# Two LoRA layers on 2048 rows: adapter numbers spread by TensorE, x1, x2 and layer 1's rows loaded ahead of A, three places for transposed x, row ends stored first with a gather of their own

## The chip, the cores and the metric

One core of a Trainium2 chip. The time is what the device takes for one execution, in microseconds; before the change it is 98.39 us, the median of 3 runs (98.32 to 98.45).

## The reference

```python
# x: (64, 32, 512) f32; itok_B_6_15: (64,), adapters 6 to 15 of 32; itok_B_3_7: (64,), adapters 3 to 7 of 8; rank 16
# layer 0
result = einsum('bsd,od->bso', x, base_weight) + base_bias
h = einsum('bsd,brd->bsr', x, lora_A_w[itok_B_6_15])
x = x + result + einsum('bsr,bor->bso', h, lora_B_w[itok_B_6_15])
# layer 1
Bx = einsum('bni,bri->bnr', x, B[itok_B_3_7])
x = x + einsum('bnr,bor->bno', Bx, A[itok_B_3_7])     # SCALING is 1
```

Each of the 64 batches has 32 rows of 512 numbers and one adapter for each layer.

## The kernel before

The 2048 rows are 16 blocks of 128 rows, that is of 4 batches. Both layers are folded into one product: with W+ = weight + identity, the result of a block is x W+^T, plus for every row a rank part of 32 columns for its batch (16 of layer 0 and 16 of layer 1). For layer 1 the factor B1 has to be applied to x W+^T; that product (`c1`) is made once at the start, and so is the product of B1 with lora_B (`g`), which carries layer 0's rank part into layer 1's.

Every fp32 value is held as a high and a low fp32r part, and each product is three matmuls (high by high, high by low, low by high). ACT writes high parts (`copy`, its line is L558), DVE low parts (`low`, L640).

For a block k TensorE does:
- `base(k)` (L394): the transposed x (`xt`, two places in turn) against W+ in two halves of 256 columns; one of the halves has 128 more columns, the block's chosen adapter rows (`select` on ACT, layers L0 and L1), so 384 columns.
- `add_gh(k)` (L432): `u_own` (on DVE, from the 128 columns, turned and masked) against `g_sel(k)`, which GpSimd selects from the gathered rows (`g_select`, L332).
- `up(k)` (L440): 6 matmuls of the rank part (`u_sel`) against `up_rows`, whose high part is `up_high` on ACT and low part `up_low` on GpSimd (L339).
Then DVE adds the bias (`finish`, L679) and SyncE (SP) stores the block.

The order of each engine is written out by hand. In the steady loop TensorE does add_gh(k-1) behind the first quarter of base(k), and up(k-1) behind base(k). add_gh(2) stands in base(3), behind up(1).

The gathered rows come from a table in DRAM, `by_rank`, of 640 rows (40 adapters by 16 ranks) of 644 numbers: 512 of lora_B or of layer 1's A (by rank), then the row's end: 128 of `g` (or of the identity, for layer 1), and one of bias times B1. `by_rank` is stored at the start by SP: four stores of lora_B (`bw_by_rank`), four of A1 (`a1_by_rank`), and one of all row ends (`row_ends`, L223), which waits for `g` and its copy on ACT. All nine count on one semaphore. GpSimd waits for all of it and issues one indirect DMA for each block (`gather`, L322), 128 rows of 2,576 bytes, 330 KB; four places (GATHERS). gather(0), (1), (2) go ahead of the loop, in which come g_select(k), up_low(k) and gather(k+3). The numbers of the rows to gather are computed on GpSimd (L291 to L314) from `ids_all`, which two DMAs spread over 128 partitions.

At the start TensorE runs 6 `keep_warm` matmuls on zeros (L362), b1's transposes, the four `w_fill` (transposes of W+, L370) with `c1_part` between them (L378), `x_fill(0)` (transposes of x, L414), lora_B's transposes (L466), x_fill(1), base(0)'s first half, the 16 matmuls of `g` (L480), the transposes of A (L487), base(1)'s second half, x_fill(2), base(0)'s second half, and so on. An fp32 matmul is counted as two by the profile, a transpose as one. base(0)'s second half is begun without the chosen columns, and `down` (L405) adds them for the first two chunks once ACT has selected them. Blocks from 3 on are transposed by DVE (`x_turn`, L647).

SP issues its DMAs in one queue, in the order written: b1, w (4), x0, lora_B, lora_A, x1, A1, x2, ids (2), bias, the nine stores, x3, then the rest of x between the stores of the output.

## Time and profile before

| | |
|---|---|
| median of the runs | 98.39 us (98.32 to 98.45) |
| the profiled execution's own time | 97.92 us |
| its span | 95.8 us |
| busy: TensorE, its weight loads | 91.5 us, 90.0 us |
| busy: DVE, ACT, GpSimd (POOL) | 64.8 us, 58.7 us, 58.0 us |
| share of TensorE in the chain that ended last | 90% |
| moved by DMA | 19.45 MB, mean 203 GB/s |

The span runs from the first instruction to the last, and the time has some 2 us more around it. The chain is followed back from the last instruction, at each step to what released it or to the instruction ahead of it on its engine.

### The profile page before, as it was taken

What the parts mean: (1) busy time and instruction counts of PE and PEld (TensorE: products, weight loads), DVE (VectorE), ACT (ScalarE), POOL (GpSimd) and SP (SyncE); (2) the same over time, 40 slices, a digit from 0 to 9 for tenths busy, and PEclk for the clock granted to TensorE, in tenths of its full rate; (3) what the DMA queues carried; (4) which work ended last, traced back from release to release, by engine and by line L of the source; (5) the groups of instructions that cost most, each with busy time, mean ns of one, the idle gap of its engine ahead of it and who ended that gap; (6) DMA issues with size and microseconds to landing.
All of it is one profiled execution on the core that took longest, in us unless ns stands there. A gap on an engine that the chain in (4) does not pass through costs nothing.

```text
span 95.8 us, 2305 instructions
## 1 busy us (share of the span) xinstructions
PE 91.5 (96%) x662; PEld 90.0 (94%) x662; DVE 64.8 (68%) x120; ACT 58.7 (61%) x189; POOL 58.0 (61%) x126
## 2 busy tenths in 40 slices
PE   5999999999999999999999999999999999999980
PEld 5899999999899998999999999999999999999970
DVE  4499799227076468959587877768595868786460
ACT  0074598874588796748494948567584949480210
POOL 6504008850568999999576584959585766808500
PEclk9999999999999999999999999999999999999998
DMA  2999998968896289989996499992836354520205
GB/s 40 312 347 387 374 403 262 281 156 214 215 224 223 53 250 238 310 249 235 203 290 218 70 319 209 238 269 91 228 44 229 34 213 54 200 110 0 110 0 219
DMA packets 16335, 19.45 MB, mean 203 GB/s; under 512 B 1444, under 2 KB 11556, under 8 KB 16164
## 3 DMA queue, kind: packets, MB, share of 16 engines
q1 hardware_dynamic: 15040, 14.04, 50.1%
q0 software_dynamic: 1280, 5.28, 22.1%
q8 instruction: 5, 0.08, 0.4%
q14 instruction: 6, 0.05, 0.3%
q10 hardware_dynamic: 4, 0.00, 0.0%
HBM read 13.47 MB, written 5.84 MB: 202 GB/s over the span
## 4 chain that ended last, share of the span: by engine, by line
PE 90%; DVE 4%; ACT 2%; issue 1%; DVEq 0%; ACTq 0%
PE psum L394 55%; PE psum L440 11%; PE psum L432 4%; PE psum L362 4%; PE psum L480 4%; PE psum L378 4%; PE psum L370 3%; DVE table_rounded L640 3%; PE psum L466 2%; PE psum L414 1%; PE psum L405 1%; PE psum L448 1%; DVE y L679 1%; ACT row_ends L558 1%; ACT table_rounded L558 1%
## 5 line engine op out<-in xcount | busy, mean ns | idle before, releaser
L394 PE MATMUL psum<-wd,xt 128*128 128x256 f32 (+1 forms) x384 | 62.3, 310 | 0.0
L394 PEld LDWEIGHTS psum<-wd,xt 128*128 128x128 f32 x384 | 56.1, 188 | 0.0
L558 ACT ACTIVATE wd<-table_rounded 128x128 fp32r x128 | 27.7, 297 | 14.7 <-PE psum L394 12.5
L339 POOL TENSOR_TENSOR up_rows<-gathered_rows,up_rows 128x512 fp32r<-128x512 f32 x16 | 20.6, 1289 | 14.0 <-ACT up_rows L558 14.0
L322 POOL DMA_INDIRECT gathered_rows<-by_rank,rows x16 | 15.9, 996 | 6.3 <-DMA by_rank<-row_ends 3.8
L640 DVE TENSOR_TENSOR xt<-psum,xt 128x512 fp32r<-128x512 f32 x16 | 11.1, 691 | 6.6 <-ACT xt L558 5.9
L647 DVE STREAM_TRANSPOSE psum<-x_squares 128x512 f32<-128x512 f32 x13 | 14.4, 1110 | 0.0
L440 PE MATMUL psum<-up_rows,u_sel 128*128 128x256 f32 x96 | 14.2, 284 | 0.0
L440 PEld LDWEIGHTS psum<-up_rows,u_sel 128*128 128x128 f32 x96 | 12.8, 190 | 0.2
L659 DVE STREAM_TRANSPOSE psum<-psum 128x128 f32<-128x128 f32 x16 | 5.3, 330 | 11.2 <-PE psum L394 7.8
L332 POOL TENSOR_TENSOR g_sel<-gathered_rows,batch_mask 128x16 f32<-128x16 f32 x64 | 12.1, 227 | 0.9 <-DMA gathered_rows<-by_rank,rows 0.7
L558 ACT ACTIVATE xt<-psum 128x512 fp32r<-128x512 f32 x16 | 9.6, 597 | 4.4 <-DVE psum L647 1.8
L679 DVE TENSOR_TENSOR y<-psum,bias_all 128x512 f32<-128x512 f32 x15 | 10.4, 692 | 1.1 <-PE psum L440 0.5
L558 ACT ACTIVATE up_rows<-gathered_rows 128x512 fp32r<-128x512 f32 x16 | 10.0, 623 | 0.0
L558 ACT ACTIVATE u_sel<-psum 128x128 fp32r<-128x128 f32 x16 | 4.2, 262 | 5.8 <-PE psum L432 5.8
L432 PE MATMUL psum<-u_own,g_sel 128*128 128x128 f32 x32 | 6.3, 279 | 0.1
L640 DVE TENSOR_TENSOR u_sel<-psum,u_sel 128x128 fp32r<-128x128 f32 x16 | 4.6, 288 | 2.3 <-ACT u_sel L558 2.3
L666 DVE SCALAR_TENSOR_TENSOR u_own<-psum,gathered_rows,batch_mask 128x128 f32<-128x128 f32 x16 | 5.6, 348 | 0.5
L432 PEld LDWEIGHTS psum<-u_own,g_sel 128*128 128x128 f32 x32 | 5.3, 188 | 0.5 <-issue 0.5
L281 POOL COPY a_by_rank<-a_rows 128x1024 f32<-128x1024 f32 x1 | 2.0, 2010 | 5.3 <-DMA a_rows<-in_L_cond_A 5.3
L362 PE MATMUL psum<-warm 128*128 128x128 f32 x16 | 3.9, 425 | 1.1 <-DVE warm L683 1.1
L362 PEld LDWEIGHTS psum<-warm 128*128 128x128 f32 x16 | 3.6, 330 | 1.1 <-DVE warm L683 1.1
(60 smaller groups left out, 72.1 us busy)
## 6 DMA issues: line engine op xcount, KB each, us to landing
out<-y SPq DMA_DIRECT2D x15, 256.0 KB
x_squares<-in_x SPq DMA_DIRECT2D x8, 256.0 KB
w_rows<-in_L_cond_base_weight SPq DMA_DIRECT2D x4, 256.0 KB, 4.0
bw_rows<-in_L_cond_lora_B_w SPq DMA_DIRECT2D x1, 1024.0 KB, 7.0
a_rows<-in_L_cond_lora_A_w SPq DMA_DIRECT2D x1, 1024.0 KB, 9.2
by_rank<-bw_by_rank SPq DMA_DIRECT2D x4, 256.0 KB
x_squares<-in_x SPq DMA_DIRECT2D x8, 128.0 KB
x_rows<-in_x SPq DMA_DIRECT2D x3, 256.0 KB, 9.3
```

What stands on the lines that cost most here:

```text
L322: nc.gpsimd.indirect_dma_start(out=gathered_rows[:, k % GATHERS, :], out_offset=None, in_=by_rank_dram[:, :], in_offset=bass.IndirectOffse ...
L332: last = nc.gpsimd.tensor_tensor(out=g_sel[:, k % 2, b, L1, :], in0=gathered_rows[:, k % GATHERS, bass.ds(n1[b] * R + G_COL, R)], in1=batc ...
L339: nc.gpsimd.tensor_tensor(out=up_rows[:, k % 2, LO, :], in0=gathered_rows[:, k % GATHERS, 0:D], in1=up_rows[:, k % 2, HI, :], op=ALU.subtr ...
L362: nc.tensor.matmul(XT[:, 0:P], warm[:, :], warm[:, :], start=True, stop=True)
L394: last = nc.tensor.matmul(bank_of(k, half)[:, start:end], xt[:, k % 2, c, x_part, :], wd[:, w_part, c, col:col + end - start], start=(c == ...
L432: nc.tensor.matmul(u_now, g_sel[:, k % 2, :, :, :], u_own[:, :], start=True, stop=True).then_inc(gh_filled, 1)
L440: last = nc.tensor.matmul(products(k)[:, half, :], u_sel[:, k % 2, u_part, :], up_rows[:, k % 2, r_part, half * HALF:(half + 1) * HALF], s ...
L558: return nc.scalar.activation(dst, src, ACT.Copy)
L640: return nc.vector.tensor_tensor(out=dst, in0=whole, in1=high, op=ALU.subtract)
L647: nc.vector.transpose(out=XT.rearrange("p (c b s) -> p b c s", c=C, b=NB), in_=x_squares[:, k * NB:(k + 1) * NB, :].rearrange("p b (i c) - ...
L666: nc.vector.scalar_tensor_tensor(out=u_own[:, :], in0=u_blocks, scalar=gathered_rows[:, k % GATHERS, BB_COL:BB_COL + 1], in1=batch_mask[:, ...
L679: nc.vector.tensor_tensor(out=y[:, k % SLOTS, :].rearrange("p (h n) -> p h n", h=2), in0=products(k), in1=bias_all[:, :].rearrange("p (h n ...
```

## The change

- The adapter numbers of both layers are scaled on one partition by DVE (`ids_scaled`) and spread over 128 partitions by one matmul with ones; the two DMAs of `ids_all` go. DVE copies the result out of PSUM, and GpSimd computes the row numbers ahead of w_chunks(3), no longer behind the bias terms.
- 5 warm-up matmuls instead of 6, the 2 fillers go. b1's copy goes from DVE to ACT, and a small ACT operation (`table_call`) stands ahead of it.
- SP loads x1 and x2 ahead of A1, and bias and A (`lora_A`) behind them.
- `xt` has three places. x_fill(2) stands ahead of the matmuls of `g`, base(2)'s first half ahead of base(0)'s second, which is now one piece of 12 matmuls of 384 columns; `down` goes.
- A row of `by_rank` is now its end first (132 numbers, 16 unused), then the 512: 660 numbers, five units of 132. `row_ends` is stored ahead of the four stores of A1, on a semaphore of its own, and block 0's ends are gathered by themselves (`first_ends`, 528 bytes a row) as soon as it has landed. gather(0) waits for the rest of the table; then g_select(0), then gather(1), (2), (3).
- up_low(0) goes from GpSimd to DVE; ACT does u_high(0) ahead of up_high(0).
- x's fifth group of blocks (4 and 5) is cut in two.

SP's queue from the bias load to x's later groups. Before:

```order
L212 DMA bias_all<-in_L0_cond_base_bias 128x512
L182 DMA by_rank<-bw_by_rank 512x1x128 [waits bw_by_rank_ready]
L182 DMA by_rank<-bw_by_rank 512x1x128 x3
L182 DMA by_rank<-a1_by_rank 128x1x128 [waits a1_by_rank_ready]
L182 DMA by_rank<-a1_by_rank 128x1x128 x3
L223 DMA by_rank<-row_ends 128x5x132 [waits act_drained,bias_b1_ready,zeros_ready]
L194 DMA x_squares<-in_x 32x4x128 x4
L194 DMA x_squares<-in_x 32x8x128 x4
```

The same place after the change:

```order
L239 DMA bias_all<-in_L0_cond_base_bias 128x512
L240 DMA a_rows<-in_L0_cond_lora_A_w 128x4x512
L213 DMA by_rank<-bw_by_rank 512x1x128 [waits bw_by_rank_ready]
L213 DMA by_rank<-bw_by_rank 512x1x128 x3
L250 DMA by_rank<-row_ends 128x5x148 [waits act_drained,bias_b1_ready,zeros_ready]
L213 DMA by_rank<-a1_by_rank 128x1x128 [waits a1_by_rank_ready]
L213 DMA by_rank<-a1_by_rank 128x1x128 x3
L225 DMA x_squares<-in_x 32x4x128 x8
```

The row ends' store has passed the four of A1, and lora_A stands behind the bias.

GpSimd at its first gathers, before (ISA rows set a register for the one behind them):

```order
L322 DMA gathered_rows<-by_rank,rows 128x644 [waits masks_ready,table_stored,ids_in,rows_ready]
L322 DMA gathered_rows<-by_rank,rows 128x644 x2
L241 TENSOR_LOAD ids
L332 ISA [waits gathered_0]
L332 TENSOR_TENSOR g_sel<-gathered_rows,batch_mask 128x16
```

and after:

```order
L379 DMA first_ends<-by_rank,first_units 128x132 [waits masks_ready,ends_stored,ids_in,rows_ready]
L355 DMA gathered_rows<-by_rank,rows 128x660 [waits table_stored]
L272 TENSOR_LOAD ids
L365 ISA [waits first_ends_gathered]
L365 TENSOR_TENSOR g_sel<-first_ends,batch_mask 128x16
L365 ISA
L365 TENSOR_TENSOR g_sel<-first_ends,batch_mask 128x16
L365 ISA
L365 TENSOR_TENSOR g_sel<-first_ends,batch_mask 128x16
L365 ISA
L365 TENSOR_TENSOR g_sel<-first_ends,batch_mask 128x16
L355 DMA gathered_rows<-by_rank,rows 128x660 x3
```

A gather has come ahead of the others, and g_select(0) stands between gather(0) and gather(1).

TensorE from base(1)'s second half to add_gh(0), before:

```order
L394 MATMUL psum<-wd,xt 128x256 x11
L414 MATMUL psum<-ident,x_rows 128x128 [waits x_loaded_2,xt_lo_ready]
L414 MATMUL psum<-ident,x_rows 128x128 x3
L394 MATMUL psum<-wd,xt 128x256 [waits dve_drained,act_drained]
L394 MATMUL psum<-wd,xt 128x256 x5
L405 MATMUL psum<-wd,xt 128x128 [waits sel1_ready,sel0_ready]
L405 MATMUL psum<-wd,xt 128x128 x5
L394 MATMUL psum<-wd,xt 128x384 x6
L394 MATMUL psum<-wd,xt 128x384 [waits sel0_ready,sel1_ready,dve_drained,act_drained]
L394 MATMUL psum<-wd,xt 128x384 x11
L394 MATMUL psum<-wd,xt 128x256 [waits xt_lo_ready,xt_hi_ready]
L394 MATMUL psum<-wd,xt 128x256 x11
```

and after:

```order
L433 MATMUL psum<-wd,xt 128x256 [waits act_drained,xt_lo_ready,xt_hi_ready]
L433 MATMUL psum<-wd,xt 128x256 x11
L433 MATMUL psum<-wd,xt 128x256 [waits act_drained,dve_drained,xt_lo_ready,xt_hi_ready]
L433 MATMUL psum<-wd,xt 128x256 x11
L433 MATMUL psum<-wd,xt 128x384 [waits sel0_ready,sel1_ready,dve_drained,act_drained]
L433 MATMUL psum<-wd,xt 128x384 x11
L433 MATMUL psum<-wd,xt 128x384 [waits sel0_ready,sel1_ready,dve_drained,act_drained]
L433 MATMUL psum<-wd,xt 128x384 x11
L462 MATMUL psum<-u_own,g_sel 128x128
```

The transposes and the six matmuls of 128 columns are gone from here, and block 2's first half stands ahead of block 0's second. The core of the diff:

```diff
-WARM_UPS = 6
-FILLERS = 2
+X_SLOTS = 3
+WARM_UPS = 5
-G_COL, BB_COL = D, D + P
-ROW = BB_COL + 4
+G_COL, BB_COL = 0, P
+ENDS = P + 4
+UNITS = 5
+ROW = UNITS * ENDS
+UP_AT = ROW - D
...
-            sp.dma_start(a_rows[:, :, :], lora_a.rearrange("(g n) r d -> (n r) g d", g=C)).then_inc(a_in, 16)
             load_x(1)
+            load_x(2)
...
-            load_x(2)
-            for layer, ids_of in ((L0, ids0), (L1, ids1)):
-                sp.dma_start(ids_all[:, layer, :, :].rearrange("p k b -> p (k b)"),
-                             ids_of.rearrange("(a k) -> a k", a=1).to_broadcast([P, B])).then_inc(ids_all_in, 16)
             sp.dma_start(bias_all[:, :], bias.rearrange("(a n) -> a n", a=1).to_broadcast([P, D])).then_inc(bias_in, 16)
+            sp.dma_start(a_rows[:, :, :], lora_a.rearrange("(g n) r d -> (n r) g d", g=C)).then_inc(a_in, 16)
...
+            sp.dma_start(by_rank_dram.rearrange("(g p) c -> p g c", p=P)[:, :, 0:UP_AT], row_ends[:, :, :]).then_inc(ends_stored, 16)
             sp.wait_ge(a1_by_rank_ready, 2)
             for c in range(C):
                 store_by_rank(sp, a1_by_rank, N1, N0 * R, c)
-            sp.dma_start(by_rank_dram.rearrange("(g p) c -> p g c", p=P)[:, :, D:ROW], row_ends[:, :, :]).then_inc(table_stored, 16)
...
+            nc.gpsimd.tensor_scalar(out=first_units[:, :], in0=row_sums[:, 0:1], scalar1=float(UNITS), scalar2=None,
+                                    op0=ALU.mult).then_inc(rows_ready, 1)
...
-            pool.wait_ge(table_stored, (2 * C + 1) * 16)
+            pool.wait_ge(ends_stored, 16)
+            nc.gpsimd.indirect_dma_start(out=first_ends[:, :], out_offset=None,
+                                         in_=by_rank_dram.rearrange("n (u c) -> (n u) c", c=ENDS),
+                                         in_offset=bass.IndirectOffsetOnAxis(ap=first_units[:, 0:1], axis=0),
+                                         ).then_inc(first_ends_gathered, 16)
+            pool.wait_ge(table_stored, 2 * C * 16)
             gather(0)
+            g_select(0)
             gather(1)
             gather(2)
-            for k in range(NBLK):
+            gather(3)
+            for k in range(1, NBLK):
...
+            pe.wait_ge(ones_ready, 1)
+            pe.wait_ge(ids_scaled_ready, 1)
+            nc.tensor.matmul(fill_of("ids")[:, 0:2 * B], ones[:, :], ids_scaled[:, :],
+                             start=True, stop=True).then_inc(filled, 1)
             w_fill(0)
-            keep_warm(FILLERS)
...
             base(0, range(C), halves=[0])
+            x_fill(2)
...
             base(1, range(C), halves=[1])
-            x_fill(2)
+            wait_x(2)
+            wait_drained(pe, "a0")
+            base(2, range(C), halves=[0])
             wait_drained(pe, "c1")
-            base(0, [0, 1], halves=[1], with_d=False, group_check=False)
             wait_d(0)
-            down(0, [0, 1])
-            base(0, [2, 3], halves=[1], group_check=False)
+            base(0, range(C), halves=[1])
...
-            wait_x(2)
-            base(2, range(C), halves=[0])
             add_gh(0)
             wait_d(2)
-            base(2, [0, 1], halves=[1])
+            base(2, range(0, C - 1), halves=[1])
             up(0)
-            base(2, [2, 3], halves=[1])
+            base(2, [C - 1], halves=[1])
...
             select(1, L0, first[1, L0])
-            xt_high(2)
             select(2, L0)
             select(2, L1)
-            up_high(0)
             xt_high(3)
             u_high(0)
+            up_high(0)
             select(3, L0)
             up_high(1)
             select(3, L1)
...
             turn_u(0)
-            xt_low(2)
+            own_u(0)
             x_turn(3)
-            own_u(0)
             xt_low(3)
             u_low(0)
             turn_u(1)
+            dve.wait_ge(up_hi_ready, 1)
+            low(up_rows[:, 0, LO, :], gathered_rows[:, 0, UP_AT:ROW], up_rows[:, 0, HI, :]).then_inc(first_up_ready, 1)
             own_u(1)
```

## Rows read from the trace of the kernel before

**Rows 1.** The page's busy time (us), share of the span, instructions.

```profile
PE 91.5 (96%) x662; PEld 90.0 (94%) x662; DVE 64.8 (68%) x120; ACT 58.7 (61%) x189; POOL 58.0 (61%) x126
```

**Rows 2.** Windows: stretch, length, busy time (instructions) by engine, PEclk, DMA share, GB/s.

```profile
36.20:92.00 55.80, 55.80 (x405) 55.80 (x406) 40.55 (x77) 35.39 (x127) 38.46 (x77) 1.00 0.69 177
```

**Rows 3.** The chain that ended last: start us, us, what.

```profile
1.12 2.93 PE psum L362 x12
...
6.73 0.89 PE psum L378 x8
...
10.85 0.48 PE psum L414 x4
...
14.06 0.72 PE psum L414 x4
14.77 1.43 PE psum L394 x12
16.20 3.58 PE psum L480 x32
...
24.21 0.30 ACT wd L558
...
25.44 4.65 PE psum L394 x30
30.09 0.24 PE psum L432 x2
...
36.19 0.46 PE psum L432 x2
```

**Rows 4.** Timeline of POOL: start us, us, line, operation [idle before it <- what ended it].

```profile
18.15 0.19 POOL L291 CAST row_of_rank_f<-row_of_rank 128x8 f32<-128x8 int32 x1
...
20.66 0.20 POOL L314 CAST rows<-row_sums 128x16 uint32<-128x16 f32 x1
24.63 1.16 POOL L322 DMA_INDIRECT gathered_rows<-by_rank,rows  x1 [3.77 <-DMA by_rank<-row_ends]
26.10 0.95 POOL L322 DMA_INDIRECT gathered_rows<-by_rank,rows  x1 [0.30 <-issue]
...
28.96 0.77 POOL L332 TENSOR_TENSOR g_sel<-gathered_rows,batch_mask 128x16 f32<-128x16 f32 x4 [0.66 <-DMA gathered_rows<-by_rank,rows]
...
31.13 0.99 POOL L322 DMA_INDIRECT gathered_rows<-by_rank,rows  x1
32.13 0.76 POOL L332 TENSOR_TENSOR g_sel<-gathered_rows,batch_mask 128x16 f32<-128x16 f32 x4
32.84 1.28 POOL L339 TENSOR_TENSOR up_rows<-gathered_rows,up_rows 128x512 fp32r<-128x512 f32 x1
34.28 0.99 POOL L322 DMA_INDIRECT gathered_rows<-by_rank,rows  x1 [0.16 <-POOL up_rows L339]
35.28 0.76 POOL L332 TENSOR_TENSOR g_sel<-gathered_rows,batch_mask 128x16 f32<-128x16 f32 x4
```

**Rows 5.** DMA issues: number, KB of one, median us from issue to landing.

```profile
b_rows<-in_L_cond_B SPq DMA_DIRECT2D x1, 256.0 KB, 2.7
```

**Rows 6.** Timeline of ACT.

```profile
19.81 0.60 ACT L558 ACTIVATE row_ends<-psum 128x512 f32<-128x512 f32 x1 [0.90 <-PE psum L480]
...
31.61 0.61 ACT L558 ACTIVATE up_rows<-gathered_rows 128x512 fp32r<-128x512 f32 x1
32.13 0.90 ACT L558 ACTIVATE wd<-table_rounded 128x128 fp32r x4
```

**Rows 7.** Timeline of TensorE: base(1)'s second half, behind A's transposes.

```profile
21.46 1.68 PE L394 MATMUL psum<-wd,xt 128*128 128x256 f32 x12
```

**Rows 8.** Timeline of SP, its DMA issues.

```profile
17.34 2.56 SPq L182 DMA_DIRECT2D by_rank<-a_by_rank  x4
20.51 0.38 SPq L223 DMA_DIRECT2D by_rank<-row_ends  x1
20.94 4.02 SPq L194 DMA_DIRECT2D x_squares<-in_x  x8
```

More of the change, by code:

```diff
@@ L171, in wait_drained, with ends, wait_ends, wait_up_rows @@
                 engine.wait_ge(dve_drained, DVE_DRAINS.index(name) + 1)
+        def ends(k, col, width):
+            if k == 0:
+                return first_ends[:, bass.ds(col, width)]
+            return gathered_rows[:, k % GATHERS, bass.ds(col, width)]
+        def wait_ends(engine, k):
+            if k == 0:
+                engine.wait_ge(first_ends_gathered, 16)
+            else:
+                engine.wait_ge(gathered[k % GATHERS], 16 * (k // GATHERS) + 16)
+        def wait_up_rows(engine, k):
+            if k == 0:
+                engine.wait_ge(first_up_ready, 1)
+            else:
+                engine.wait_ge(up_ready, k)
         def chunk(rows_of, c):
@@ L457, in _ @@
             c1_part(1)
+            wait_drained(pe, "ids")
             w_fill(3)
@@ L717, in _, with lay_bw @@
             xt_low(0)
-            for q in range(4):
+            def lay_bw(q):
                 wait_filled(dve, f"bw{q}")
```

147 lines of the change are left out of this document (79 added, 68 removed).

## The prediction

> **What bounds the kernel now.** I read first the page's busy shares: TensorE is busy for 96% of the span [rows 1]. Then its share after the start: from 36.2 us to 92.0 it is busy for all of 55.80 us [rows 2], so no other engine and no transfer costs anything there, and that stretch keeps its order. What the change can move is the time at which it begins, that is the third add_gh, at 36.19 us in the chain that ended last [rows 3]. So the question is one number: where does that matmul land afterwards?
>
> The same chain tells what comes before it [rows 3]. TensorE runs nearly without a hole, but slowly at first: 12 warm-up passes take 2.93 us (0.24 each), while 8 passes from 6.73 us on take 0.89 (0.111 each). x_fill(1) takes 0.72 where another x_fill takes 0.48, so it waits 0.24 for x1 at 14.06; and the chain leaves TensorE at 19.79 for ACT and DVE, to come back from the adapter selection at 24.51.
>
> Last, GpSimd's timeline from 24.63 to 36.04 us, which the chain doesn't show [rows 4]. GpSimd waits for the store of row_ends, then works almost solidly: three gathers, a wait of 0.66 for the first to land, and then g_select, up_low and gather in turn. g_select(2) ends at 35.28 + 0.76 = 36.04, and add_gh(2), which reads it, begins at 36.19. So TensorE fully loaded and GpSimd fully loaded arrive at that point together: an earlier TensorE alone buys nothing there.
>
> **The change part by part.** The sum is made against the profiled execution (97.92 us, of which 95.8 are the span). The median of the runs is 98.39, 0.47 above it; I add each difference to the median.
>
> Start of TensorE. One warm-up (2 passes) and two fillers (4) go, one matmul for the ids (2) comes: 4 passes fewer. They should leave no hole: b1 lands 2.7 us after its issue [rows 5], and 10 slow passes from 1.12 last until 3.6. They come out of the end of the slow part, so I price them at the fast 0.111: -0.44 (at the slow 0.24 it would be -0.98, and nothing if TensorE's faster passes began later by as much). x1 now goes ahead of the 1 MB of A, so its 0.24 goes. x_fill(2) comes ahead of the row-end matmuls: +0.48; what hides its wait is that xt_low(1) is put ahead of the last bw copy on DVE. The row ends' copy on ACT, at 19.81 for 0.60 [rows 6], moves by -0.44 - 0.24 + 0.48 = -0.20.
>
> Selection and the merged block. From 21.46 us [rows 7] TensorE now has 24 matmuls of 256 columns (0.119 each, 12 in 1.43) and 24 of 384 (18 of them in 4.65 - 1.43, so 0.179 each): 2.86 + 4.30 = 7.16 us instead of 30.09 - 21.46 = 8.63 [rows 3, 7]. base(2)'s first half fills what was a wait for select(0, L0): that ends at 24.51 - 0.20 = 24.31, TensorE gets there at 21.26 + 2.86 = 24.12, so 0.2 of waiting stays. add_gh(0) could start at 28.6 instead of 30.09: 1.5 us earlier. The third place for transposed x and the ids by TensorE cost nothing else: the small GpSimd operations on the row numbers (18.15 to 20.86 us, 2.7 in all [rows 4]) move ahead of w_chunks(3); begun at about 5.7, behind the ids' copy on DVE, they end at 8.6 with the one that is new, and leave 2.7 us for one copy before TensorE has done x_fill(0) at 10.85 + 0.48 [rows 3].
>
> The gathers. This is where it is given back. The store of row_ends is issued at 20.51 and GpSimd's first gather starts at 24.63 [rows 4, 8], 4.12 later. With the copy 0.20 earlier the same store frees GpSimd at 24.43. What stood before this store, the stores of a1, now stands behind it, with x3 and x4 (8 issues took 4.02 us [rows 8]) after them; the a1 stores take 2.56 us to issue [rows 8] and still land before GpSimd is through with the ends gather. That gather comes first: it starts at 24.43, and its landing is e later. The full gather(0) goes out behind it, at no cost, under the wait. But g_select(0) now stands ahead of gather(1), where before gather(1) followed gather(0) by 1.47 us [rows 4]. So gather(1) starts at 24.43 + e + 0.76 (g_select) + 0.15 (the gap of gathers behind GpSimd's work) and lands g later, and g_select(1) waits for it, which it did not before: it ran at 32.13, at once behind gather(3).
>
> Neither e nor g stands in the trace by itself. For g the nearest row is the first gather of the same 330 KB: start 24.63, g_select at 28.96 after its wait, 4.33. Below it is bounded by the 256 KB load of b1, 2.7 from issue to landing; above I allow 4.7. I take 4.33. For e, 66 KB instead of 330, the bounds are 2.7 and the 4.33 of the full one; I take 2.8, near the small one, because four fifths of the bytes are gone. Then gather(1) lands at 24.43 + 2.8 + 0.91 + 4.33 = 32.47.
>
> From its landing there are two ways to add_gh(2). By GpSimd: from g_select(1)'s start to g_select(2)'s end is 36.04 - 32.13 = 3.91, with 0.15 to TensorE [rows 4]: 36.6 with the wait's release. By ACT, which also stood free of gather(1) before: up_high(1) 0.61 and select(3, L1) 0.90 [rows 6] plus 0.1, then base(3) chunk 0 (0.90), up(1) (6 x 0.119 = 0.72) and chunk 1 (0.90) on TensorE: 32.47 + 4.13 = 36.6 as well. So add_gh(2) comes at 36.6 instead of 36.19: +0.4 us. The 1.5 us that TensorE gained turn into waits at up(0), add_gh(1), base(3) and add_gh(2), about 1.9 in all. up_low(0), moved to DVE, takes 1.28 off GpSimd, but the time is spent waiting for the landing of gather(1).
>
> What the Trainium skill makes of e: its page "DMA: Bandwidth & Descriptors", section "Anatomy of one DMA — SWDGE (gpsimd) path", gives a DMA a fixed cost of about 2.0 us whatever its size, plus the bytes at 436 GB/s. So a gather of a fifth of the rows is hardly shorter. As an estimate by that page, with the generation times of the rows (1.16 and 0.95) ahead, e is 1.16 + 2.0 + 0.15 = 3.3 and g 0.95 + 2.0 + 0.78 = 3.7; the sum e + g is 7.0 against my 7.13, and the result +0.3. For the first gather that page gives 3.9 where the row has 4.33.
>
> **The rivals.** All are one formula: add_gh(2) = 24.43 + e + g + 5.04; it is level with before at e + g = 6.7.
> Faster, 97.9: the gathers land sooner. Below e + g = 6.5 the kernel is faster, and what then holds it is GpSimd's own order: ends gather 1.46 with its gap, gather(0) 0.95, g_select 0.76, three gathers 3 x 1.25, so g_select(1) at 31.5 at the earliest, 0.6 ahead of 32.13, and 97.8. For it: after the changed start fewer x loads run beside gather(1), while the 4.33 was measured among them. Against it: the single measured landing.
> Level, 98.4: e + g between 6.5 and 6.9, or the start gains 0.3 to 0.4 more than I give it because the slow passes are the ones saved.
> The whole of TensorE's gain stays, 96.9: the row_ends store would have to free GpSimd 1.9 us sooner than I say. Nothing in the rows shows its 4.12 us held up by what was ahead of it, so I give it little.
> Much slower, 99.6 and over: e near the 4.33 of a full gather, which is 1.5 us more: 100.3.
>
> **How the numbers follow.** Slower as forecast, 98.8: 0.50 (0.06 of it over 99.5). Level: 0.24. Faster by gathers that land early: 0.22; the whole gain: 0.04. This kernel's runs can tell about 0.2% (0.2 us) from no change, so faster 0.26, same 0.24, slower 0.50. The forecast is 98.39 + 0.41 = 98.8. Its own range is 98.6 to 99.5; with the other cases up to the limit of GpSimd's order, 97.8 to 99.5.
>
> **What would show it.** TensorE ready for add_gh(0) at about 28.6; row_ends' copy at about 19.6 and GpSimd's ends gather at about 24.4; g_select(0) at 27.2 and gather(1) at 28.1; g_select(1) not behind gather(3) without a gap, but after a wait for gathered_rows, at about 32.5; up_high(1) on ACT at the same time; add_gh(2) at 36.6, and after it no idle TensorE and the same 55.8 us. I am wrong if g_select(1) follows gather(3) with no wait, if the ends gather starts well before 24.4, or if TensorE still has new holes after add_gh(2).

## The result, and the profile after

| | before | changed |
|---|---|---|
| median of the runs, same chip | 98.42 us (98.32 to 98.57, 4 runs) | 99.95 us (99.25 to 101.38, 4 runs) |
| ratio to before | | 1.0137 [1.0090, 1.0183] |
| the profiled execution's own time, its span | 97.92, 95.8 us | 99.41, 97.6 us |
| start of add_gh(2) | 36.19 us | 37.31 us |
| from there to add_gh(15), the last | 54.63 us | 55.23 us |

Slower, as forecast, but by 1.5 us instead of 0.4, and outside the range. In the profiles two things make up the difference: add_gh(2) came 0.7 us later than forecast, and the loop after it takes 0.6 us more (forecast: the same). A third, which neither of these two profiles shows, lifts many executions of the changed kernel by up to 2 us more. Against the three stands 0.25 us that the changed kernel takes less outside the span (1.86 on the mean against 2.11), which the forecast did not have.

The medians are over all executions, while the ratios leave out those more than 1.5% above the same kernel's fastest, which takes away most of the upper cluster where the times of a kernel fall into two, so each range is given beside its ratio.

The page's busy times of the changed kernel, as [rows 1]:

```profile
PE 92.0 (94%) x652; PEld 89.3 (92%) x652; DVE 65.3 (67%) x122; ACT 60.9 (62%) x191; POOL 58.7 (60%) x127
```

Windows, as [rows 2], but with TensorE's columns alone: stretch, length, busy time (instructions), PEclk, DMA share, GB/s. 1.39 us of holes before the loop, none in it.

```profile
24.60:38.20 13.60, 12.21 (x74) 1.00 0.72 199
38.20:94.00 55.80, 55.80 (x404) 1.00 0.72 180
```

The chain that ended last, as [rows 3]:

```profile
1.70 4.42 DMA w_rows<-in_L_cond_base_weight
6.47 0.69 DVE w_chunks L746
7.52 0.75 PE psum L410 x4
...
15.62 0.73 PE psum L444 x4
16.35 3.76 PE psum L516 x32
20.14 0.61 ACT row_ends L594
20.84 2.93 DMA by_rank<-row_ends
23.84 0.81 issue
24.66 3.38 DMA first_ends<-by_rank,first_units
29.22 3.63 DMA gathered_rows<-by_rank,rows
34.61 1.06 PE psum L433 x6
...
45.80 2.64 PE psum L433 x18
```

Where before TensorE alone led to add_gh(2), now the store of the row ends and the two gathers do. The loop's pieces come behind them.

POOL's timeline, as [rows 4]:

```profile
24.66 1.19 POOL L379 DMA_INDIRECT first_ends<-by_rank,first_units  x1 [8.42 <-DMA by_rank<-row_ends]
26.15 0.95 POOL L355 DMA_INDIRECT gathered_rows<-by_rank,rows  x1 [0.30 <-issue]
28.23 0.75 POOL L365 TENSOR_TENSOR g_sel<-first_ends,batch_mask 128x16 f32<-128x16 f32 x4 [1.13 <-DMA first_ends<-by_rank,first_units]
29.22 0.99 POOL L355 DMA_INDIRECT gathered_rows<-by_rank,rows  x1 [0.24 <-issue]
...
33.04 0.58 POOL L365 TENSOR_TENSOR g_sel<-gathered_rows,batch_mask 128x16 f32<-128x16 f32 x3 [0.33 <-DMA gathered_rows<-by_rank,rows]
33.79 0.22 POOL L365 TENSOR_TENSOR g_sel<-gathered_rows,batch_mask 128x16 f32<-128x16 f32 x1 [0.16 <-issue]
```

The order of the forecast: g_select(0) waits for the small gather, gather(1) goes out only behind it, and g_select(1) waits for gather(1).

ACT's timeline, as [rows 6]:

```profile
20.14 0.60 ACT L594 ACTIVATE row_ends<-psum 128x512 f32<-128x512 f32 x1 [1.36 <-PE psum L516]
...
32.88 0.63 ACT L594 ACTIVATE up_rows<-gathered_rows 128x512 fp32r<-128x512 f32 x1 [0.92 <-DMA gathered_rows<-by_rank,rows]
```

TensorE's timeline at add_gh(0), up(0), add_gh(1) and add_gh(2):

```profile
25.09 4.40 PE L433 MATMUL psum<-wd,xt 128*128 128x384 f32 x24 [0.20 <-ACT wd L594]
29.33 0.38 PE L462 MATMUL psum<-u_own,g_sel 128*128 128x128 f32 x2
...
31.94 0.98 PE L470 MATMUL psum<-up_rows,u_sel 128*128 128x256 f32 x6 [0.45 <-DVE up_rows L682]
...
34.15 0.46 PE L462 MATMUL psum<-u_own,g_sel 128*128 128x128 f32 x2 [0.70 <-POOL g_sel L365]
...
37.31 0.46 PE L462 MATMUL psum<-u_own,g_sel 128*128 128x128 f32 x2
```

add_gh(0) starts 0.76 earlier than before [rows 3] and waits for nothing; then the waits eat it up. The last of them is add_gh(1)'s, and from 34.15 to 37.31 TensorE has no wait.

### The profile page after: what moved, and what is told of

It is laid out like the page before. It is cut to its first block, busy times and chain, and to the rows that moved or that the text cites. A ratio compares the mean times of both kernels' runs of the same rounds, so it can differ in the third digit from the quotient of the medians.

```text
span 97.6 us, 2294 instructions
## 1 busy us (share of the span) xinstructions
PE 92.0 (94%) x652; PEld 89.3 (92%) x652; DVE 65.3 (67%) x122; ACT 60.9 (62%) x191; POOL 58.7 (60%) x127
## 4 chain that ended last, share of the span: by engine, by line
PE 75%; DMA 15%; issue 2%; DVE 2%; POOL 1%; SPq 1%; ACT 1%; DVEq 0%; POOLq 0%
PE psum L433 49%; PE psum L470 11%; DMA w_rows<-in_L_cond_base_weight 5%; PE psum L462 4%; PE psum L516 4%; DMA gathered_rows<-by_rank,rows 4%; DMA first_ends<-by_rank,first_units 3%; DMA by_rank<-row_ends 3%; PE psum L418 3%; PE psum L501 2%; PE psum L444 2%; POOL g_sel L365 1%; PE psum L410 1%; DVE w_chunks L746 1%; DVE w_rows L738 1%
## 5 line engine op out<-in xcount | busy, mean ns | idle before, releaser
L433 PE MATMUL psum<-wd,xt 128*128 128x256 f32 (+1 forms) x384 | 63.0, 313 | 0.2 <-ACT wd L594 0.2
L433 PEld LDWEIGHTS psum<-wd,xt 128*128 128x128 f32 x384 | 56.8, 189 | 0.6 <-issue 0.4
L372 POOL TENSOR_TENSOR up_rows<-gathered_rows,up_rows 128x512 fp32r<-128x512 f32 x15 | 19.4, 1290 | 14.1 <-ACT up_rows L594 14.1
L470 PEld LDWEIGHTS psum<-up_rows,u_sel 128*128 128x128 f32 x96 | 12.8, 189 | 0.8 <-DVE up_rows L682 0.8
L365 POOL TENSOR_TENSOR g_sel<-gathered_rows,batch_mask 128x16 f32<-128x16 f32 x60 | 11.4, 226 | 1.3 <-DMA gathered_rows<-by_rank,rows 0.9
L379 POOL DMA_INDIRECT first_ends<-by_rank,first_units x1 | 1.2, 1186 | 8.4 <-DMA by_rank<-row_ends 8.4
L682 DVE TENSOR_TENSOR table_rounded<-psum,table_rounded 128x512 fp32r<-128x512 f32 x5 | 3.2, 682 | 2.7 <-ACT table_rounded L594 2.7
L418 PE MATMUL psum<-b_cols,w_chunks 128*128 128x128 f32 x32 | 4.2, 275 | 0.0
```

What stands on the lines that cost most here:

```text
L365: last = nc.gpsimd.tensor_tensor(out=g_sel[:, k % 2, b, L1, :], in0=ends(k, n1[b] * R + G_COL, R), in1=batch_mask[:, b, 0:R], op=ALU.mult)
L372: nc.gpsimd.tensor_tensor(out=up_rows[:, k % 2, LO, :], in0=gathered_rows[:, k % GATHERS, UP_AT:ROW], in1=up_rows[:, k % 2, HI, :], op=ALU ...
L418: last = nc.tensor.matmul(fill_of("c1")[:, c * P:(c + 1) * P], w_chunks[:, oc, c, :], b1_cols[:, oc, :], start=(oc == 0 and c == 0), stop= ...
L433: last = nc.tensor.matmul(bank_of(k, half)[:, start:end], xt[:, k % X_SLOTS, c, x_part, :], wd[:, w_part, c, col:col + end - start], start ...
L470: last = nc.tensor.matmul(products(k)[:, half, :], u_sel[:, k % 2, u_part, :], up_rows[:, k % 2, r_part, half * HALF:(half + 1) * HALF], s ...
L682: return nc.vector.tensor_tensor(out=dst, in0=whole, in1=high, op=ALU.subtract)
```

## The experiments

None of these kernels leaves out a part of the reference. The ratios are to the kernel before, timed beside each. A pass is a matmul as the profile counts it. "Late passes" is said of an execution in which TensorE's passes keep twice their later length until 9 to 10 us. Three dots in a diff or a list of rows stand for lines left out.

### First: is it the gathers, the addresses, chance?

**a_again** is the changed kernel unedited.

> The changed kernel as it is, once more, for its spread: its first four runs lay between 99.25 and 101.38 us, those of the kernel before between 98.32 and 98.57. If the spread belongs to the kernel, the five lie over 1 us apart again, and above 99.2; if it was the chip of that day, they lie within 0.3 us, near 99.3.

Measured: 100.46 us (99.48 to 101.92, 8 executions), ratio 1.0214 [1.0180, 1.0248]; seven of the eight are over 100.1 and the profiled one, 99.48, is the fastest. So both profiles of this program show one of its best executions. The kernel before stays between 97.66 and 99.2 in 22 executions beside this one. In all 96 that were timed beside the experiments, three lie above 99.3 (99.4, 100.21, 100.84), so long executions exist there too, but are rare.

**a_g1first** issues gather(1) ahead of g_select(0):

```diff
             gather(0)
-            g_select(0)
             gather(1)
+            g_select(0)
```

> The changed kernel with gather(1) ahead of g_select(0). Theory (the wait for the first ends holds gather(1) back): gather(1) starts at about 27.4 instead of 29.2 us, its data is used by 31.5, g_select(0) ends at about 29.2, in time for TensorE at 29.3, and add_gh(2) comes at 36.0 or earlier instead of 37.3: 1.0 to 1.5 us faster than the changed kernel. Rival (the extra gather itself, in front of all others, costs the time): less than 0.3 us.

Measured: ratio 1.0078 [1.0033, 1.0123], median 100.15, but 98.47 to 101.98, in two clusters (six executions at 98.47 to 99.21, seven from 100.15). The lower cluster begins 0.8 us under the changed kernel's lowest, 99.25. The profile fell on the longest execution and so shows one of the upper cluster. TensorE in it, from the ids' matmul on:

```profile
4.62 0.79 PE L484 MATMUL psum<-ids_scaled,ones 1*128 1x128 f32 x2
5.34 1.13 PE L410 MATMUL psum<-ident,w_rows 128*128 128x128 f32 x4
6.26 1.91 PE L418 MATMUL psum<-b_cols,w_chunks 128*128 128x128 f32 x8
7.97 1.91 PE L410 MATMUL psum<-ident,w_rows 128*128 128x128 f32 x8
```

and in the 99.41 execution of the changed kernel:

```profile
4.46 0.48 PE L484 MATMUL psum<-ids_scaled,ones 1*128 1x128 f32 x2
4.87 0.75 PE L410 MATMUL psum<-ident,w_rows 128*128 128x128 f32 x4
5.46 1.06 PE L418 MATMUL psum<-b_cols,w_chunks 128*128 128x128 f32 x8
```

Eight passes take 1.91 us in the one and 1.06 in the other (a group's length holds its last pass's whole latency). From start to start a pass takes 0.214 us in the one (6.26 to 7.97) and 0.111 in the other. The factor of two is that between the clock's levels of 1.2 and 2.4 GHz, but the windows' PEclk is 1.00 in both, so the clock is read from the lengths alone. TensorE comes to the last w_fill at 10.79 us instead of 9.00, 1.8 late. The ends' gather starts at 27.27 us, not 24.66, so 0.8 us of its delay came after that point.

**b_pad512** moves every buffer of the kernel before from w_rows on by 512 bytes, `wd` (W+ and the selected columns) among them, to where the changed kernel has it:

```diff
+        pad = sb("pad", [P, P])
         w_rows = sb("w_rows", [P, C, D])
```

> The kernel before with one unused tile of 512 bytes a partition ahead of w_rows, so that all tiles behind it lie where the changed kernel has wd: the matmuls of 384 columns took 173 to 180 ns there and 7 less before. If the place of wd matters, a block takes 4.46 us instead of 4.39 and the kernel about 0.8 us more. If the place of xt and the tiles behind it matters (their place within 512 bytes is not changed here), or the three places of xt, nothing changes: 98.4.

Measured: 98.41 (97.65 to 100.19), ratio 0.9991 [0.9958, 1.0024]. This shift of `wd` costs nothing.

**a_xt512** moves `xt`, and the buffers behind it, in the changed kernel; `wd`, which stands ahead, stays. `xt` goes from byte 192128 of a partition (128 behind a multiple of 256) to 192512 (a multiple of 512, as before the change):

```diff
+        pad = sb("pad", [P, 96])
         xt = sb("xt", [P, X_SLOTS, C, 2, P], F32R)
```

> The changed kernel with 384 unused bytes ahead of xt, so that xt, up_rows and u_sel begin at a multiple of 512 bytes again, as in the kernel before; wd stays where the change put it. If the place of xt matters, a block takes 4.39 us again instead of 4.46 and the kernel is 0.7 to 0.8 us faster than the changed kernel. If that of wd matters, no difference.

Measured: 100.32 (99.84 to 102.02), ratio 1.0168 [1.0131, 1.0206]. The profiled execution, 100.64, has the late passes (the ends' gather at 26.45), so the time can't be read against the other. But the loop can be read by itself: from add_gh(2) at 39.03 to add_gh(15) at 93.76 it is 54.73 us instead of 55.23, with the address alone changed. b_xt128 and a_ids_xt below show the same in the times.

### Second: are the missing warm-ups the cause? They aren't

**a_warm** gives the changed kernel its sixth warm-up and the two fillers back; **b_cold** takes them from the kernel before:

```diff
 # a_warm
-WARM_UPS = 5
+WARM_UPS = 6
+FILLERS = 2
...
             w_fill(0)
+            keep_warm(FILLERS)
 # b_cold
-WARM_UPS = 6
-FILLERS = 2
+WARM_UPS = 5
+FILLERS = 0
```

> The changed kernel with the six warm-up matmuls and the two fillers back, nothing else. In the profiles of a_g1first and a_xt512 TensorE's passes stay at 0.21 us until about 10 us, in those of the changed kernel and a_again they are at 0.11 from 5.5 us on; in the kernel before from 6.5 us on. Theory: without the fillers the start is too thinly filled and the fast passes begin in some executions 3.4 us later, 1.7 us lost. Then this one has no executions above 100.2 and its median is near 99.5 (0.3 to 0.5 us over the changed kernel's best, for six passes more). Rival (the spread has another source, the ids' matmul or the queue): the executions lie between 99.2 and 102 as before and the median stays at 100.4.

Measured: 100.31 (99.23 to 102.62), ratio 1.0153 [1.0106, 1.0200]: the spread is all there.

> The kernel before with five warm-ups and no filler, the only edit. If the fillers are what makes the fast passes begin in time, some executions are 1 to 1.7 us slower, the spread goes beyond 1.5 us and the median above 98.8. If not, 98.3 to 98.5, as before, or a little less.

Measured: 98.66 (97.89 to 99.62), ratio 1.0017 [0.9975, 1.0059]. The spread, 1.7 us, is as wide as the theory asked, the median is not as high, and a_warm kept its long executions. So the missing warm-ups are not the cause, though b_cold's six executions leave open whether they add to the spread. Nor is it all in the passes: a_warm's profiled execution, 100.55, has them short from 5.4 us on, and its add_gh(2) at 38.44; gather(1)'s rows are first used 4.4 us after its start instead of 3.7.

**a_warm_xt_g1** is a_warm with the pad and gather(1) ahead of g_select(0). **a_warm_xt_noends** is a_warm with the pad and the row ends' part undone:

```diff
-            sp.dma_start(...[:, :, 0:UP_AT], row_ends[:, :, :]).then_inc(ends_stored, 16)
             sp.wait_ge(a1_by_rank_ready, 2)
             for c in range(C):
                 store_by_rank(sp, a1_by_rank, N1, N0 * R, c)
+            sp.dma_start(...[:, :, 0:UP_AT], row_ends[:, :, :]).then_inc(table_stored, 16)
...
-            pool.wait_ge(ends_stored, 16)
-            nc.gpsimd.indirect_dma_start(out=first_ends[:, :], ...)
-            pool.wait_ge(table_stored, 2 * C * 16)
+            pool.wait_ge(table_stored, (2 * C + 1) * 16)
             gather(0)
-            g_select(0)
             gather(1)
             gather(2)
-            gather(3)
...
```

g_select(0) then reads the gathered rows, and x_turn(3) stands ahead of own_u(0) on DVE, as before the change.

> As a_warm, with xt at a multiple of 512 bytes and gather(1) ahead of g_select(0). The place of xt gives back 7 ns for each matmul of 384 columns, 0.08 us a block, 0.8 to 1.0 in all (shown by the rows of a_xt512, not by its time). Of the order of the gathers: if g_select(0)'s wait ahead of gather(1) is what costs, 0.6 to 1.0 us more, so 97.7 to 98.1 in all; if the gathers' data are what everything waits for, g_select(1) waits for gathered_rows as in a_g1first, and it is 98.5 or more.

Measured: 100.41 (98.42 to 101.35), ratio 1.0065 [1.0010, 1.0121].

> As a_warm, with xt at a multiple of 512 bytes, and the part with the row ends undone: row_ends stored behind the a1 stores on the one semaphore, no gather of the first ends, gather(0), (1), (2) ahead of g_select(0). up_low(0) stays on DVE, and all of TensorE's order stays changed. If the gather of its own costs more than the rest of the change gives, gather(0) starts at about 24.5, g_select(0) ends at 29.5, add_gh(2) comes at about 35.4 and the time is 97.6, faster than before. If the ends' part helps, it is slower than a_warm_xt_g1.

Measured: median 100.71; 97.83 and 98.07, then four from 100.65 to 101.15; ratio 0.9960 [0.9917, 1.0003], by the first two alone. In both profiled executions (98.42 and 98.07) add_gh(2) is at 37.00 and 36.66: the better executions follow the gathers. The others, in both kernels 1.4 to 3.3 us above, come whichever gather goes first; so what makes them is elsewhere. None of them was profiled.

### Third: the matmul with one active row, and the address

**a_ids128** makes the sums of the ids' matmul over 128 rows, 127 of them zero:

```diff
-        ids_scaled = sb("ids_scaled", [1, 2 * B])
-        ones = sb("ones", [1, P])
+        ids_scaled = sb("ids_scaled", [P, 2 * B])
+        ones = sb("ones", [P, P])
...
+            nc.vector.memset(ids_scaled[:, :], 0.0).then_inc(ones_ready, 1)
...
-            nc.vector.tensor_scalar(out=ids_scaled[:, :], ...)
+            dve.wait_ge(ones_ready, 2)
+            nc.vector.tensor_scalar(out=ids_scaled[0:1, :], ...)
```

> The changed kernel with the matmul that spreads the adapter numbers made over 128 rows instead of one: ids_scaled has 128 partitions, zero but for the first, and ones is [128, 128]; the sums are the same. In the executions of the changed kernel that last 100 us and more TensorE's passes of the filling stay at about twice their later length until 10 us (6.26 1.91 x8 in the run with gather(1) first), in the others only until 5.2 to 5.5 us. Theory: the matmul with a single active row, which stands among the first passes, is what keeps the passes long in some executions. By it they are short from about 5.5 us in each execution, the median falls to about 99.3 us and the spread to under 0.5 us. Rival: the late change comes from something else in the changed start (the later landing of w's rows, the order of the loads): the times still go from 99.2 to 102, with a median of 100 to 100.5.

Measured: 99.44 (99.32 to 99.72, 6 executions), ratio 1.0079 [1.0049, 1.0109]. The spread fell from 2.4 us to 0.4. TensorE in it:

```profile
4.51 0.63 PE L484 MATMUL psum<-ids_scaled,ones 128*128 128x128 f32 x2
4.94 0.77 PE L410 MATMUL psum<-ident,w_rows 128*128 128x128 f32 x4
5.55 1.06 PE L418 MATMUL psum<-b_cols,w_chunks 128*128 128x128 f32 x8
```

The same sums with all rows active, and short passes behind them. The other executions have no profile, but by their times none has late passes.

**a_noids** undoes the whole part: two DMAs of `ids_all` ahead of the bias, scaled on DVE, the row numbers computed behind the bias terms on GpSimd as before.

```diff
+            for layer, ids_of in ((L0, ids0), (L1, ids1)):
+                sp.dma_start(ids_all[:, layer, :, :]..., ids_of....to_broadcast([P, B])).then_inc(ids_all_in, 16)
             sp.dma_start(bias_all[:, :], ...)
...
-            nc.tensor.matmul(fill_of("ids")[:, 0:2 * B], ones[:, :], ids_scaled[:, :],
-                             start=True, stop=True).then_inc(filled, 1)
```

> The changed kernel with the first of its parts undone: the adapter numbers come to all partitions by two DMAs as before the change, are scaled on VectorE, and TensorE spreads nothing. Theory that the spreading matmul is what makes the passes stay long in some executions: median about 99.3 us, spread under 0.5 us, the row_ends copy at 20.0 us and the ends' gather about 24.6. Rival, that the cause lies elsewhere in the start: times from 99.2 to 102 as before. By both theories the steady loop is that of the changed kernel (4.46 us a block), so that the time is not under 98.9.

Measured: 100.76 (99.55 to 101.24), ratio 1.0149 [1.0095, 1.0203]. Missed. In its profiled execution (101.02) the passes are short from 5.5 us and the row_ends copy is early, at 19.84; what is late is its store. The chain that ended last:

```profile
19.84 0.61 ACT row_ends L592
20.55 5.24 DMA by_rank<-row_ends
25.85 0.81 issue
26.67 2.69 DMA first_ends<-by_rank,first_units
```

5.24 us instead of 2.93. The two DMAs of 32 KB stand ahead of the bias and of lora_A's 1 MB in SP's queue, and lora_A took 12.8 us from issue to landing (9.8 in a_ids128); it lands beside the row ends' store. That the one delays the other is read from one trace, not tried. Four of the six executions are above 100.6 without any one-row matmul. So this run neither supports nor refutes it; it shows a second way to lose 2 us.

**b_xt128** puts 128 bytes ahead of `xt` in the kernel before, which moves the buffers behind `xt` too:

```diff
+        pad = sb("pad", [P, S])
         xt = sb("xt", [P, 2, C, 2, P], F32R)
```

> The kernel before with 128 bytes per partition put ahead of the transposed x alone, so that it starts 128 bytes behind a multiple of 256, as in the changed kernel. Theory: the start of the transposed x in SBUF sets how long the 384-column matmuls take. By it a block takes 4.46 us instead of 4.39, add_gh(14) starts 52.5 us behind add_gh(2) instead of 51.9, and the ratio is 1.008. Rival: the longer matmuls of the changed kernel come from its three places for x, or from the other order of the work, not from the address: 4.39 us a block and a ratio of 1.000.

Measured: 99.41 (98.59 to 99.83), ratio 1.0084 [1.0052, 1.0117]. The chain in b_xt128, three blocks apart, and the same in the kernel before:

```profile
40.32 2.64 PE psum L395 x18
...
53.70 2.64 PE psum L395 x18
```

```profile
40.21 2.58 PE psum L394 x18
...
53.41 2.59 PE psum L394 x18
```

A block is (53.70 - 40.32) / 3 = 4.46 us instead of 4.40. In the changed kernel it is 4.46 too, with 18 matmuls in 2.64. That it is `xt` and not a buffer behind it is told by which matmuls got longer: those of 384 columns, which read `wd` and `xt`, follow each other by 176 ns instead of 169 (medians from 40 to 88 us), while those of `up` (119) did not. All 19 profiles agree: from add_gh(2) to add_gh(15) it is 55.23 or 55.24 us in the seven kernels with `xt` 128 bytes behind a multiple of 256, and 54.55 to 54.74 in the twelve with it at a multiple of 512.

### Fourth: the causes one by one

**b_onerow** adds one matmul with one active row to the kernel before. Nothing waits for it.

```diff
             last.then_inc(filled, 1)
+            nc.tensor.matmul(XT[:, 0:P], warm[0:1, :], warm[0:1, :], start=True, stop=True)
             w_fill(0)
```

> The kernel before with one matmul more behind the transposes of b1's rows: 1x128 by 1x128, one active row, as the one that spreads the adapter numbers in the changed kernel. Nothing waits for it. Theory that such a matmul early in the start is by itself what keeps the passes long until 10 us in some executions: the times go from about 98.4 to 100.5 and more, with a median of 99 or above. Rival, that it takes something else of the changed start beside it (five warm-up matmuls instead of six and no fillers, the two scaled sets of numbers awaited on TensorE, the loads' order): the times stay within 97.7 to 99.3, median 98.4 to 98.7, as the kernel before.

Measured: 99.76 (99.26 to 100.14, 6 executions), ratio 1.0151 [1.0107, 1.0195]. TensorE and GpSimd in it:

```profile
4.83 0.79 PE L451 MATMUL psum<-warm 1*128 1x128 f32 x2
5.55 1.13 PE L370 MATMUL psum<-ident,w_rows 128*128 128x128 f32 x4
6.48 1.06 PE L362 MATMUL psum<-warm 128*128 128x128 f32 x4
7.33 1.91 PE L378 MATMUL psum<-b_cols,w_chunks 128*128 128x128 f32 x8
```

```profile
26.24 1.16 POOL L322 DMA_INDIRECT gathered_rows<-by_rank,rows  x1 [5.14 <-DMA by_rank<-row_ends]
```

The matmul itself is 0.7 us in TensorE's order (4.83 to 5.55); the passes behind it stay long to about 9.4 us, where before the change they were short from about 6.5. TensorE comes to the last w_fill 1.74 us later than before (11.05 instead of 9.31), of which some 1.0 us is the late passes, and the first gather starts 1.6 us later than the 24.63 of [rows 4]. One matmul that nobody waits for makes the whole kernel 1.5% longer: all six executions are above 99.2, where 22 of the 27 of the kernel before beside them are under 99.1. The same addition made over 128 rows was not run on the kernel before; of the changed kernel a_ids128 is that comparison.

**a_ids_xt** has both mended, the 128 rows and the pad.

> The changed kernel with two side effects taken out: the spreading matmul over 128 rows, and the transposed x at a multiple of 512 bytes. By the theory that these two are all that the forecast lacked, beside 0.3 us of the start: a block takes 4.39 us, the ends' gather starts at 24.8, add_gh(2) at 37.3, and the median is 98.8 to 98.9 us (99.44 less 0.6), with a spread under 0.5 us. Rival, that the two don't add (the late passes come back with another placing, as in the run with the aligned x alone): median above 99.5.

Measured: 98.97 (98.42 to 99.12, 10 executions), ratio 1.0049 [1.0020, 1.0078]; the spread is 0.7, not under 0.5. With add_gh(2) at 36.90 and add_gh(15) at 91.53, the loop takes its 54.63 us again:

```profile
36.90 0.46 PE L463 MATMUL psum<-u_own,g_sel 128*128 128x128 f32 x2
```

**a_ids_xt_g1** and **a_ids_xt_noends** are the same with gather(1) ahead of g_select(0), and with the row ends' part undone (edits as above).

> As the changed kernel with both side effects taken out, and gather(1) issued ahead of g_select(0). Theory: add_gh(2) hangs on gather(1)'s landing, which moves 1 us forward less what the two gathers in flight cost each other (it took 4.6 us instead of 3.7 in an earlier run with this order): add_gh(2) at 37.0, median 98.5. Rival, that the two gathers delay each other by the whole of what is gained: 98.8. If the landing keeps its 3.7 us: 97.8.

Measured: 98.25 (97.85 to 98.64), ratio 0.9990 [0.9964, 1.0016]. GpSimd's timeline:

```profile
24.75 1.19 POOL L380 DMA_INDIRECT first_ends<-by_rank,first_units  x1 [8.80 <-DMA by_rank<-row_ends]
...
27.50 0.95 POOL L356 DMA_INDIRECT gathered_rows<-by_rank,rows  x1 [0.30 <-issue]
28.47 0.75 POOL L366 TENSOR_TENSOR g_sel<-first_ends,batch_mask 128x16 f32<-128x16 f32 x4
...
32.21 0.96 POOL L366 TENSOR_TENSOR g_sel<-gathered_rows,batch_mask 128x16 f32<-128x16 f32 x4 [0.59 <-DMA gathered_rows<-by_rank,rows]
```

gather(1) starts 1.7 us earlier than in the changed kernel and takes 4.7 us to its first use instead of 3.7. add_gh(2) stays where it was, at 36.89; the 0.7 us of the medians is not to be seen in it.

> As the changed kernel with both side effects taken out, and the row ends' part undone: the ends' store after A's, one count for all stores, g_select(0) from gathered_rows. Theory: gather(0) starts at 25.1, lands 4.1 us later, add_gh(2) follows at 36.6, and the median is 98.1, 0.7 us under the same kernel with the ends' part. Rival, that the ends' part costs nothing beside the side effects: the same 98.8 in both.

Measured: 98.13 (97.80 to 98.84), ratio 0.9970 [0.9941, 0.9999]. The ends' part costs 0.8 us as it stands (98.97 against 98.13, on one chip).

### Fifth: a better kernel

Both take a_ids_xt_noends or a_ids_xt_g1 and move x_fill(2) behind `g`, with its copies on ACT and DVE:

```diff
 # TensorE
             base(0, range(C), halves=[0])
-            x_fill(2)
...  the 16 matmuls of g
+            x_fill(2)
 # ACT: xt_high(2) from ahead of the selections to behind the copy of row_ends
 # DVE: xt_low(2) from behind table 1's low half to ahead of table 0's; lay_bw(3) ahead of xt_low(1)
```

> The changed kernel with both side effects taken out, the row ends' part undone, and x_fill(2) moved: on TensorE from ahead of the g product to behind it, its copy on ScalarE behind the row_ends copy, its low half on VectorE ahead of table 0's low halves, and lay_bw(3) ahead of xt_low(1). Theory that the row_ends copy and with it the first gather come 0.7 us earlier: gather(0) at 24.3. TensorE's work up to add_gh(2) is then what binds, as only 0.2 to 0.6 us of waits are left there (30.06 to add_gh(0) with 0.35, 25.15 with 0.20): add_gh(2) at 36.2 instead of 36.6, median 97.7. Rival, that the work moved onto the way of table 0's copies costs ScalarE and VectorE as much as it gives: 98.1, as without the move.

Measured: 98.06 (97.56 to 99.70), ratio 0.9974 [0.9941, 1.0007]: no gain. In its profile the store of row_ends goes out 0.95 us earlier but takes 4.12 us to land instead of 3.23, so gather(0) starts at 24.96, where it was.

> The same move with the ends' own gather kept and gather(1) issued ahead of g_select(0). Theory that the last wait ahead of add_gh(2) is gather(1)'s landing: the ends' gather at 24.0, add_gh(0) at 29.3, add_gh(2) at 36.4, median 97.9 (98.25 in the same kernel without the move). Rival, that TensorE's own work sets it there: no gain from the move, 98.2.

Measured: 97.71 (97.34 to 97.96), ratio 0.9928 [0.9898, 0.9958]: faster than before the change by 0.7%, and the best of all. In the two profiles little of that shows: add_gh(2) is at 36.13 instead of 36.19 and the span is 95.7 instead of 95.8, since the profiled execution of the kernel before (97.92) was one of its fast ones. GpSimd and TensorE in it:

```profile
23.96 1.19 POOL L380 DMA_INDIRECT first_ends<-by_rank,first_units  x1 [8.26 <-DMA by_rank<-row_ends]
```

```profile
36.13 0.38 PE L463 MATMUL psum<-u_own,g_sel 128*128 128x128 f32 x2
```

## Why the prediction was off, step by step

**What bounds.** Right: add_gh(2) was the place. But "that stretch keeps its order", and so its 55.8 us, was the first step that failed. A stretch in which TensorE is busy throughout has no waits to lose, yet its matmuls can get longer: with `xt` 128 bytes behind a multiple of 256, 18 of them take 2.64 us instead of 2.59, and with the rest of the block that is 0.6 us from add_gh(2) to add_gh(15) (55.23 - 54.63). "The third place for transposed x and the ids by TensorE cost nothing else" is the sentence that put both side effects at nothing. For the transposed x the cost isn't in the third place but in where the buffer then began: a_xt512 and a_ids_xt take it away in the changed kernel, b_xt128 brings it into the kernel before.

**Start of TensorE.** Forecast: row_ends' copy at 19.61. Measured 20.14, 0.53 late. base(0) ended at 15.62 instead of 15.52, with a wait of 0.28 at the third w_fill, which had to wait for DVE's work on its rows; x_fill(2) cost 0.73 instead of 0.48, and `g` 3.76 instead of 3.58 [rows 3]. The store then freed GpSimd in 3.82 us (20.84 to 24.66) instead of 4.12 [rows 4, 8], so the ends' gather came only 0.23 late. And I priced the matmul for the ids at two fast passes. This is the step with the largest error: in the profiled executions with late passes (a_g1first, a_xt512, b_onerow) TensorE is 1.7 to 1.8 us behind at the last w_fill, and with the matmul over 128 rows the ratio falls from 1.0214 (a_again) to 1.0079 (a_ids128).

**Selection and the merged block.** Forecast: add_gh(0) possible at 28.6, 1.5 earlier. It started at 29.33, unhindered, 0.76 earlier: 0.5 of the missing 0.7 is the start's delay. It didn't matter.

**The gathers.** e was 3.57 instead of 2.8 (24.66 to 28.23), g 3.66 instead of 4.33 (29.22 to 32.88). Both off by 0.7, with opposite signs, so the sum, 7.23, was close to my 7.13; that part of the forecast held partly by luck. The nearest row misled in both: four fifths fewer bytes made the ends' gather only 0.76 shorter than the first gather of [rows 4], and gather(1), of the full size, was 0.67 shorter than that first one. The Trainium skill's page "DMA: Bandwidth & Descriptors", section "Anatomy of one DMA — SWDGE (gpsimd) path", with its fixed cost whatever the size, had given 3.3 and 3.7 as estimates: of e the trace agrees better with that rule than with my row, and on g it agrees. But a fixed price for g doesn't hold in every run: with gather(1) issued 1.7 us earlier, g is 4.7 (a_ids_xt_g1), and in a_warm, with the order of the changed kernel, 4.4.

**The tail.** From the landing to add_gh(2) 4.43 instead of 4.13. It goes neither by select(3, L1) nor by g_select(2), but through g_select(1), which ends 1.13 behind the landing, to add_gh(1) at 34.15, and then TensorE's own work of 3.16 between add_gh(1) and add_gh(2), of which the loop's longer matmuls are a part. I had two ways to add_gh(2) in the sum and left out the third, which ended last. add_gh(2): 0.23 (start) + 0.18 (e, g and the gap) + 0.30 (tail) = 0.71 over the 36.6 of the forecast.

**The sum.** Profile to profile: +1.12 at add_gh(2), +0.60 in the loop, and 0.08 behind add_gh(15) make the span's 1.8. The times of these two executions differ by only 1.49, because less lies outside the span. The median is 0.54 us above the profiled execution, and 0.98 in a_again, where in the kernel before it is 0.47. With the two side effects out (a_ids_xt) the ratio is 1.0049, where my 98.8 was 1.0042. So the mechanism that I forecast is there, and it is 0.5% of the 1.4 to 2.1%. That the number agrees so closely is partly luck: in a_ids_xt's profile add_gh(2) is at 36.90 and not 36.6, and the span is 0.8 longer than before and not 0.4, while 0.15 us less lies outside it on the mean.

**The rivals.** The gathers that land sooner, and the level case: no, e + g was over 7. The whole gain: no. "Much slower, e near 4.33" would have given a time near the measured one for a reason that isn't there.

**The marks.** Right: g_select(1) behind a wait (33.04), up_high(1) at the same landing (32.88), no idle TensorE after add_gh(2). Wrong: "the same 55.8 us" behind it. None of the three signs by which I would be wrong came, because none of them looks at the length of a pass, which is what both side effects changed. Late: the row_ends copy, g_select(0) (28.23, forecast 27.2), gather(1) (29.22, forecast 28.1).

**Still open.** Why some executions of one program have the late passes and others not: none of the profiles tells. They are in three of the eight profiles with a one-row matmul and in none of the eleven without. With the matmul over 128 rows 6, 10, 12, 12 and 8 executions of the changed kernel's relatives have a spread of 0.4 to 1.0 us. But long executions without a one-row matmul exist too: two of twelve in best_noends (99.64, 99.70; its profiled store of row_ends landed late) and in b_pad512 (99.76, 100.19), three of 96 of the kernel before. None of these was profiled, so what they are isn't known. In a_warm and a_noids part of the loss is a late gather or store, and what is in the way of those DMAs wasn't isolated.

## What to carry to other kernels

A full engine isn't a constant one: after a change of buffers compare the time of one steady block before and after, and look at where the matmuls' operands now start. A tiny operation on the busiest engine has to be priced by what it does to the operations behind it, and executions that spread by 2% say that one profile isn't the kernel. A small gather put ahead of a big one costs its whole latency to whatever is queued behind the instruction that waits for it: issue the next transfer first, then wait.

## What the runs showed of the hardware

- A single 1x128 by 1x128 fp32 matmul among TensorE's first passes can keep the passes at twice their later length for about 3 us more in b_onerow and 4.5 in a_g1first: eight took 1.91 us instead of 1.06, until 9.4 and 10 us, where they were short from 6.5 (the kernel before) and 5.5 us on (the changed kernel). The factor is that of the clock's levels, 1.2 and 2.4 GHz, though the profile's granted clock is 1.00 throughout. TensorE was busy from 1.1 us on, ahead of that matmul and behind it. Over 128 rows it did not happen: in a_ids128, in the five kernels built on it and in the five without such a matmul (the one before, b_pad512, b_cold, b_xt128, a_noids), each profiled execution has short passes from 7.5 us at the latest. The Trainium skill's page "TensorE: Matmul & The Clock Gate", section "What's actually happening", has the number of slow matmuls at the start vary from run to run of one kernel. The clusters of a_g1first (98.47 to 99.21, 100.15 to 101.98) would fit that, but no kernel here has profiles both with and without late passes.
- Matmuls of 384 columns in fp32r take longer when the transposed x, their other operand, starts at 128 bytes behind a multiple of 256: 176 ns apart instead of 169, and 4.46 us a block instead of 4.40, 0.6 to 0.8% of the whole kernel. A shift of `wd`, the operand with the columns, by 512 bytes changed nothing.
- An indirect gather of 128 rows of 528 bytes takes 3.57 us from its start to its first use, one of 128 rows of 2,640 bytes 3.66, when issued 3 us behind the one ahead of it (3.5 to 3.7 in six profiles). Issued 1.25 us behind it, the large one took 4.6 to 4.8 us in three profiles (a_warm_xt_g1, a_ids_xt_g1, best_g1) and 5.4 in a_g1first. Distance is not all: in a_warm it took 4.4 at 3 us.
